# Attention tiles of a fused kernel: expert logits and ranks moved one tile later, and the inverse root interleaved with the expert choice

## The reference, cut to what matters

```
x = x + L0_xattn(layernorm(x), ctx)          # x: (4, 512, 512), ctx: (4, 1024, 512)
x = x + L0_ffn(layernorm(x))
# L1_xattn: attention of the tokens over the 1024 context rows, keys = values = ctx
scores  = einsum('bsd,bmd->bsm', layernorm(x), ctx) / sqrt(512)
attn    = softmax(where(mask, scores, -1e30))
x = x + einsum('bsm,bmd->bsd', attn, ctx)
# L1_ffn: mixture of 32 experts, the best 8 for each token
logits  = layernorm(x) @ gate_kernel                      # (2048, 32)
weights, chosen = top_k(softmax(logits), 8)
weights = weights / sum(weights)
x = x + sum over chosen of weight * (silu(h @ gate_e) * (h @ up_e)) @ down_e
```

## Time and profile before

| what | value |
|---|---|
| median of 3 runs | 1487.23 us (1486.8 to 1488.82) |
| profiled execution | 1489.98 us, span 1488.2 us |
| TensorE busy | 1392.3 us, 94% of the span |
| VectorE busy | 1026.7 us, 69% |
| ScalarE busy | 505.0 us, 34% |
| GpSimd busy | 383.3 us, 26% |
| mean granted TensorE clock | 0.974 of full speed |

### The profile page before, as it was taken

The page is one execution under the profiler, slowest core; times in us unless marked ns, Lnnn a source line. Parts: engine busy times, 40 slices in busy tenths (PEclk is TensorE's granted clock), DMA queues, the critical chain, the costliest instruction groups (busy, mean ns, idle before and its releaser), DMA issues.

```text
span 1488.2 us, 26995 instructions
## 1 busy us (share of the span) xinstructions
PE 1392.3 (94%) x7525; PEld 755.8 (51%) x7526; DVE 1026.7 (69%) x2467; ACT 505.0 (34%) x916; POOL 383.3 (26%) x313
## 2 busy tenths in 40 slices
PE   4899999999999999998998749999999999999996
PEld 3344444444444444444444326666666666666664
DVE  7879857976985556686766546666666666666664
ACT  0444543443435343422222113333333333333332
POOL 1000000000000000034555543353434444344443
PEclk9899999999999999999999969999999999999998
DMA  9976776766767787746666768989999988999786
GB/s 372 370 277 197 258 259 210 246 196 206 241 209 227 231 275 268 260 150 240 211 240 228 274 239 207 231 212 255 247 239 246 224 227 229 240 225 218 156 149 84
DMA packets 132696, 345.04 MB, mean 232 GB/s; under 512 B 15008, under 2 KB 19616, under 8 KB 125728
## 3 DMA queue, kind: packets, MB, share of 16 engines
q1 hardware_dynamic: 73488, 206.72, 41.2%
q0 software_dynamic: 34640, 85.74, 25.4%
q10 hardware_dynamic: 24512, 51.89, 10.9%
HBM read 192.68 MB, written 151.62 MB: 231 GB/s over the span
## 4 chain that ended last, share of the span: by engine, by line
PE 72%; DVE 11%; DMA 5%; issue 3%; another core or an unknown queue 3%; ACT 2%; SPq 2%; ACTq 1%; DVEq 0%; POOLq 0%
PE PS L1636 18%; PE PS L1634 18%; PE PS L1635 18%; PE PS L1894 5%; PE PS L1923 2%; PE PS L1922 2%; DMA CST<-in_kv 2%; DMA split_experts<-HT 2%; PE PS L1911 1%; PE PS L1588 1%; PE PS L1912 1%; DMA BIG<-in_wdT 1%; PE PS L1777 1%; ACTq L104 1%
## 5 line engine op out<-in xcount | busy, mean ns | idle before, releaser
L587 POOL DMA_INDIRECT out<-BIG,EX x159 | 247.2, 1555 | 354.1 <-issue 200.1
L1634 PE MATMUL PS<-BIG 128*128 (+1 forms) x795 | 269.0, 338 | 4.8 <-DVE BIG L1535 2.6
L1635 PE MATMUL PS<-BIG 128*128 (+1 forms) x795 | 269.0, 338 | 0.0
L1636 PE MATMUL PS<-BIG 128*128 (+1 forms) x795 | 268.9, 338 | 0.0
L1634 PE MATMUL PS<-HT,BIG 128*128 128x512 f16 (+1 forms) x512 | 194.1, 379 | 3.3 <-DVE HT L1063 1.4
L1635 PE MATMUL PS<-HT,BIG 128*128 128x512 f16 (+1 forms) x512 | 194.0, 379 | 0.0
L1636 PE MATMUL PS<-HT,BIG 128*128 128x512 f16 (+1 forms) x512 | 194.0, 379 | 0.0
L560 POOL DMA_INDIRECT rows_by_expert<-HT,POS x128 | 124.6, 973 | 135.0 <-DVE POS L1359 100.6
L823 ACT ACTIVATE BIG<-PS 128x256 f16<-128x256 f32 x159 | 61.1, 384 | 243.6 <-PE PS L1912 218.5
L1636 PE MATMUL PS<-BIG,EX 128*128 128x512 f16 (+1 forms) x376 | 143.2, 381 | 0.0
L1635 PE MATMUL PS<-BIG,EX 128*128 128x512 f16 (+1 forms) x376 | 143.2, 381 | 0.0
(11 more groups left out here) (264 smaller groups left out, 2258.2 us busy)
## 6 DMA issues: line engine op xcount, KB each, us to landing
BIG<-rows_by_expert ACTq DMA_DIRECT2D x159, 280.0 KB
HT<-in_experts SPq DMA_DIRECT2D x64, 640.0 KB, 4.8
BIG<-split_experts SPq DMA_DIRECT2D x32, 1152.0 KB
split_experts<-HT SPq DMA_DIRECT2D x96, 320.0 KB, 2.2
CST<-in_kv SPq DMA_DIRECT2D x64, 256.0 KB, 4.9
split_context<-RT SPq DMA_DIRECT2D x64, 256.0 KB, 4.7
BIG<-split_context SPq DMA_DIRECT2D x7, 2048.0 KB
rows_by_expert<-X SPq DMA_DIRECT2D x32, 280.0 KB
```

Source lines behind the costliest of these rows:

```text
L587: pool.indirect_dma_start(a_out, bass.IndirectOffsetOnAxis(ap=IDY[:, u % V:u % V + 1], axis=0), yt[u % V], None, compute_op=ALU.add).then_ ...
L1634: mm(out, lh, rh, start=first, stop=False)
L1635: mm(out, lh, rl, start=False, stop=False)
L1636: return mm(out, ll, rh, start=False, stop=last_group)
```

## The change

It takes no operation away and adds none; it changes where they stand, and one bank.

1. On TensorE `logits(t - 2)` stands right behind `probs(t)`, and `rank(t - 2)` behind `scores(t + 1)`. Both were in iteration t with index t - 1, behind parts of `readout(t)`. `query_tile(t + 4)` moves from ahead of the scores to behind the second readout chunk, and `router_tile(t - 1)` from the second to the fourth.
2. The query transposes go to bank 4, one of the two banks of the probabilities. `probs` now waits for `query_lo` of the iteration before.
3. On VectorE the choice of tile t - 2 is interleaved with the inverse root of iteration t (`tile_root_and_choose`). The places follow `scores_max`, `query_lo` moves to the end of the iteration.
4. On ScalarE `router_exp(t - 2)` and `exp_tile(t + 1)` stand ahead of `query_hi` and `router_hi`.
5. On GpSimd the last three tiles (they were two) scatter four experts each first and the other four in turn, and LANDED rises from 48 to 64.

```diff
-LANDED = 48
+LANDED = 64
...
-            scatter_rows(NT - 2, range(4))
-            scatter_rows(NT - 1, range(4))
+            for t in range(NT - 3, NT):
+                scatter_rows(t, range(4))
             for w in range(4, TOPK):
-                scatter_rows(NT - 2, (w,))
-                scatter_rows(NT - 1, (w,))
+                for t in range(NT - 3, NT):
+                    scatter_rows(t, (w,))
...
             for t in range(NT - 1):
                 probs_hi(t)
-                if t + QA < NT:
-                    query_hi(t + QA)
...
+                if t > 1:
+                    router_exp(t - 2)
+                exp_tile(t + 1)
+                if t + QA < NT:
+                    query_hi(t + QA)
                 if t:
                     router_hi(t - 1)
-                exp_tile(t + 1)
-                if t:
-                    router_exp(t - 1)
...
+            def tile_root_and_choose(m, n, cols, t):
+                tile_root_start(m, n, cols)
+                logits_scale(t)
+                tile_root_half(m, cols, 0)
+                top8(t)
+                tile_root_square(m, cols, 0)
+                top8_replace(t)
+                tile_root_refine(m, cols, 0)
+                select(t)
...
             for t in range(NT - 1):
                 if t:
-                    readout_add(t - 1)
-                    if t > 1:
-                        place(t - 2)
+                    readout_scale(t - 1)
+                    readout_sum(t - 1)
...
                 probs_lo(t)
-                if t + QA < NT:
-                    query_lo(t + QA)
-                if t or query:
-                    tile_root(t + 1, stats, slice(0 if t else 1, 2 if query else 1))
+                if t > 1:
+                    tile_root_and_choose(t + 1, stats, cols, t - 2)
+                else:
+                    tile_root(t + 1, stats, cols)
...
                 scores_max(t + 1)
+                if t > 1:
+                    place_first(t - 2)
+                    place(t - 2)
...
+                if t + QA < NT:
+                    query_lo(t + QA)
                 if t:
                     router_lo(t - 1)
-                    choose(t - 1)
...
             for t in range(NT - 2):
                 probs(t)
-                if t + QA < NT:
-                    query_tile(t + QA)
+                if t > 1:
+                    logits(t - 2)
                 scores(t + 1, range(2) if t else range(1, 2))
+                if t > 1:
+                    rank(t - 2)
...
                 readout(t, range(2))
+                if t + QA < NT:
+                    query_tile(t + QA)
+                readout(t, range(2, 4))
                 if t:
                     router_tile(t - 1)
-                readout(t, range(2, 6))
-                if t:
-                    logits(t - 1)
-                readout(t, range(6, KEYC))
-                if t:
-                    rank(t - 1)
+                readout(t, range(4, KEYC))
```

More of the change, by code:

```diff
@@ L837, in load_tile @@
                 act.dma_start(xg[u], block).then_inc(s_xg[u], 16)
-            for t in range(NT - ZN, NT - 2):
+            for t in range(NT - ZN, NT - 3):
                 act.wait_ge(s_ids[t % ZN], scatters_of(t + ZN))
@@ L1016, in tile_root @@
                 v.tensor_scalar(half, var, -0.5, None, ALU.mult).then_inc(s_nw, 1)
[L1017 to L1023, removed]
@@ L1024, in tile_root, with tile_root_half, tile_root_square @@
-                dve.wait_ge(s_nw, steps + NEWTON)
+            def tile_root_half(m, cols, i):
+                half, y, work = (nw[:, j, cols] for j in range(1, 4))
+                dve.wait_ge(s_nw, (ROUNDS + m) * NEWTON + (4 + 3 * i))
+                v.tensor_tensor(work, y, half, ALU.mult).then_inc(s_nw, 1)
+            def tile_root_square(m, cols, i):
+                y, work = (nw[:, j, cols] for j in range(2, 4))
+                dve.wait_ge(s_nw, (ROUNDS + m) * NEWTON + (5 + 3 * i))
+                v.tensor_tensor(work, work, y, ALU.mult).then_inc(s_nw, 1)
@@ new lines, in tile_root_refine, with tile_root @@
+            def tile_root_refine(m, cols, i):
+                y, work = (nw[:, j, cols] for j in range(2, 4))
+                dve.wait_ge(s_nw, (ROUNDS + m) * NEWTON + (6 + 3 * i))
+                v.scalar_tensor_tensor(y, work, 1.5, y, ALU.add, ALU.mult).then_inc(s_nw, 1)
+            def tile_root(m, n, cols):
+                tile_root_start(m, n, cols)
+                for i in range(3):
+                    tile_root_half(m, cols, i)
+                    tile_root_square(m, cols, i)
+                    tile_root_refine(m, cols, i)
+                dve.wait_ge(s_nw, (ROUNDS + m + 1) * NEWTON)
@@ new lines, in tile_root_and_choose @@
+            def tile_root_and_choose(m, n, cols, t):
+                tile_root_start(m, n, cols)
+                logits_scale(t)
[5 more added lines that the diff above has]
+                select(t)
+                tile_root_half(m, cols, 1)
+                tile_root_square(m, cols, 1)
+                tile_root_refine(m, cols, 1)
+                selected_sum(t)
+                tile_root_half(m, cols, 2)
+                selected_inverse(t)
+                tile_root_square(m, cols, 2)
+                routing_weights(t)
+                tile_root_refine(m, cols, 2)
+                dve.wait_ge(s_nw, (ROUNDS + m + 1) * NEWTON)
@@ L1811, in probs @@
                 wait(pe, s_ptl, t)
+                wait(pe, s_qlo, min(t, NT - QA))
                 for c in range(KEYC):
@@ L1856, in _ @@
             probs(a)
+            logits(a - 2)
             scores(b)
+            rank(a - 2)
             pe.wait_ge(s_ptl, a + 1)
             pe.wait_ge(s_xr, a)
-            readout(a, range(2))
+            readout(a, range(4))
             router_tile(a - 1)
-            readout(a, range(2, 5))
-            logits(a - 1)
+            readout(a, range(4, 5))
             last_probs()
             readout(a, range(5, 7))
+            logits(a - 1)
+            readout(a, range(7, KEYC))
+            pe.wait_ge(s_ptl, NT)
+            readout(b, range(2))
             rank(a - 1)
-            readout(a, range(7, KEYC))
-            for n in range(2):
-                pe.wait_ge(s_ptl, NT + n)
-                readout(b, range(4 * n, 4 * n + 4))
+            readout(b, range(2, 4))
+            pe.wait_ge(s_ptl, NT + 1)
+            readout(b, range(4, KEYC))
             router_tile(a)
```

33 lines of the change are left out of this document (14 added, 19 removed).

## The result

The changed kernel takes 1477.44 us (median of four runs, 1475.99 to 1479.46) against 1488.03 us of the kernel before beside it (1486.8 to 1490.23): ratio 0.9928, 95% interval 0.9909 to 0.9948, 10.6 us less. The profiled execution took 1476.12 us, 13.9 less than that of before. The forecast was 27.1 us less, 1460 us.

A forecast was written before the change was run, and what follows sets the result against it. Bound: a 15.07 us loop of GpSimd scatters and late TensorE signals, not TensorE. Iterations save 27.1 us, last tiles 0: 1489.98 - 27.1 = 1462.9 profiled, median 2.75 lower, so 1460 us; range 1449 to 1479.

The forecast's parts named there:

- TensorE's wait: Attention stage, before the rank: 25.3 us in 13 waits for VectorE's selection, to be covered by the scores with 1.4 to spare.
- a new ring: Attention loop: if the scores' signal always came with the last scatter, scatter, signal, maximum and places would repeat every 13.7 us.
- a rival: Attention loop, smaller gain: lateness spreads to more signals, 14.2 us an iteration, 13 us less, 1474; chance 2 in 10.
- The iteration: Attention loop: between 12.54 and 13.7 us, middle 13.1 taken; twelve iterations 156.3 instead of 183.44 us, 27.1 less.
- The last tiles: Probabilities 14 to expert stage: 3 us saved against 2.6 to 5.1 for four more scatters; net -0.6 to +1.9, taken as 0.
- The 3 us that the last places should have come earlier: After probabilities 14: fewer TensorE waits, VectorE free for the last readout sum at 20.3 us instead of 23.5.
- no long wait in front of L1339: VectorE's wait for the logits at about 4.1 us: signalled near 1.6, or 3.8 if 2.4 late, so costs nothing.
- the idle time in front of `scores_max`: VectorE, attention loop: expected to idle here for the scores' signal, which falls into the scatters and may come 2 us late.
- the bank of the query transposes at nothing: Bank 4 on TensorE: `query_lo` hands it back at 10.8 us, wanted at 12.7; cost zero, 1.9 us of cover.
- root and interleaved choice: VectorE, each iteration: root's start 0.7 us, then choice and root interleaved about 2.3, SEL written at 5.3.
- The rival "slower": Attention loop: logits' signal waits for the previous tile's last scatter; 16.5 us an iteration, 15 us more, 1502; chance 1 in 12.
- the way out of the ring: Old attention loop: first scatter, late logits' signal, places, next first scatter take 15.07 us; the new order was to shorten this.

The follow-up runs named there:

- The half bursts: Changed kernel and kernel before, tiles 0 to 3 in bursts of four scatters: 12.48 us an iteration beside them, 13.72 beside whole ones; old order mostly 13.35, then 15.2.
- The burst in two: Kernel before plus shared register addition, tiles 0 to 12: six scatters at once, last two when the next logits' signal is there: 1459.73 us, ratio 0.98.
- six and two: Changed kernel plus shared register addition, tiles 0 to 11: six scatters at once, last two when the next scores' signal is there: 1469.54 us, ratio 0.987.

## Why the prediction was wrong

The direction was right, and so was the mechanism: TensorE's wait goes, and late signals then make a new ring. The size was too large, 27 instead of 11 us, by two terms. That 1477.44 us lies inside the range (1449 to 1479) is no merit of the forecast: that end of the range was there for a rival.

**The iteration.** The step that failed: "the later the places, the earlier the next scores fall in the scatters, and then they aren't late. So an iteration lies between 12.54 and 13.7; I take the middle, 13.1." The two ends were right (12.48 where nothing is held, 13.7 as the ring), but the loop didn't stay between them: it passed through 12.96 once and then kept to 13.7. Once the scores are sent so late behind the first scatter (those sent 8.9 us behind it came at 11.5, and in other runs some sent at 7.0 and 8.0 at 11.4), their signal comes with the burst's end, and the places made from it start the next burst so that the next scores again are sent 8.9 us behind it. The ring locks at its full length, and nothing in this loop pulls it back. The half bursts show both states in one trace. Measured for iterations 2 to 13: 163.7 us where I had 156.3, 7.4 more. The collision with the memset, which I hadn't looked for, adds 2.7 in iteration 12, but the next one is 12.40 instead of 13.7; by the run with the memset moved its net is 1.2. The other 6.2 are the ring, with iterations 2 and 3, still short of it, counted in.

**The last tiles.** "So the net is -0.6 to +1.9; I take 0": it was +7.9. The four more scatters cost the whole 5.1 that I had as their upper bound: the expert stage began 4.1 us behind the start of the last scatter (864.84 to 868.94). The 3 us that the last places should have come earlier became 2.4 later, as the rank's signal of tile 13 came 4.4 us late and those of the last readout and the router transposes 7.7 and 2.6 (both there at 834.5 to 834.6); 0.4 more is the drain. I had seen such lateness at that place before (2.54 us in front of the logits) and had taken it over unchanged, while more signals now fall into the scatters there.

27.1 less, minus 7.4 and 7.9, is 11.8, which the traces have between iteration 2 and the expert stage. The two errors add up; nothing cancels.

**Right were:** hardly a wait of TensorE for SEL (one, 1.1 us); no long wait in front of L1339, which stands at 726.45 inside the choice, though the logits' signal came 1.9 us late (covered by `probs_lo`, as put); the idle time in front of `scores_max`; the bank of the query transposes at nothing; scatters 1.28 us apart; TensorE's clock at 1.00 in the iterations of 13.7. **Not right:** the first scatter, 11.3 us behind the probabilities instead of 9 (708.90 to 720.17), the late signal's 2.2; root and interleaved choice, 4.4 us (725.84 to 730.24) instead of 0.7 + 2.3, of which 1.5 are waits for VectorE's own signals; the last places at 844.90 instead of 834, and ScalarE's start of the expert stage at 868.94 instead of 855. The rival "slower" failed because the logits' signal, sent 3.7 us behind the first scatter, didn't wait for the last one: it came at 4.2 to 7.0.

Most of all, the forecast took the new order as the way out of the ring. The burst in two shows that the wait for the selection was a symptom: in the old order it goes by itself, at 13.06 us an iteration and without the longer end.

**Open:** why the signals are held. Bursts of GpSimd's scatters are needed for it, since shorter or split bursts end it in both orders, while the iteration is 13.7 us at every DMA share beside them (0.42 to 0.93). But a burst isn't enough: in the changed kernel's last one, twenty scatters from 840.59 on, TensorE's signals sent 4.3, 6.2 and 13.6 us behind the first scatter were all there within 0.02 us, and in the old order the scores' signal, sent 4.5 us behind it, was prompt too. Whether the writing of descriptors, their landing in the queues or the semaphore path is at fault, and what else has to be going on, no run here tells apart. Nor did any run take the move of the query transposes to bank 4, or that of the logits alone, out of the change.

## What to carry to other kernels

- When an engine waits for a result that had been computed some us ago ("remote" in front of it, the source's end well before), look at what else is running, not at the order of the work: here a pause in GpSimd's scatters brought 30 us in the old order and 12 in the new one, and the reordering alone 11.
- This loop, with a late signal in it, settled at the full length of its ring. Where a forecast has two states, ask which one feeds itself instead of taking the middle, and test it by making the burst short in some iterations.
- Work that moves one tile later is paid for at the end: count what then stands behind the last result, at its upper bound.

## What the runs showed of the hardware

- While GpSimd issues indirect DMAs back to back (1.28 us apart), signals of TensorE can come late. By the semaphore records of the changed kernel's loop those sent within 3.4 us of the first of eight scatters are prompt; those of the logits, sent at 3.7, come mostly at 5.66 us, some at 4.2 and one at 7.04; those of the scores (8.9) at 11.5. The arrivals lie about 1.4 us apart, more than the 1.28 between issues. In the old order the router transposes' signal, sent at 6.2, mostly came at 7.0 to 7.1. These are no fixed rule of the time since the first scatter: see the prompt signals under "Open".
- VectorE's signals to itself are held too: in the changed kernel L1027, which ended at 728.84, was signalled at 730.05, and L1032 idled 1.09 us for it.
- In the changed kernel's loop what is held to the end comes 1.5 to 1.6 us behind the end of the last scatter. With six and two, the scores' signal was sent 1.5 to 2.3 us behind the end of the burst before it and came within 0.02 us in ten iterations. A pause of 1.04 us between two bursts wasn't enough: the changed kernel's last readout, sent at 826.88, was signalled at 834.54, behind the second burst.
